# A four-stage transformer kernel: moving sums, centring, decay and gates of its linear attention between engines

## What is computed

```python
xx = xprev - x                                  # x is the layernormed input
mix_in = tanh((x + xx * time_maa_x) @ time_maa_w1)
mrg, mwa, mk_, mv_ = einsum('btfd,fdc->fbtc', mix_in..., time_maa_w2)
xrg = x + xx * (time_maa_rg + mrg)              # and xwa, xk, xv in the same way
r, k, v = xrg @ Wr.T, xk @ Wk.T, xv @ Wv.T
w = -softplus(-(time_decay + tanh(xwa @ decay_w1) @ decay_w2)) - 0.5
g = tanh(xrg @ gate_w1) @ gate_w2
kk = normalise per head (k + tanh(xk @ kkk_w1) @ kkk_w2)
a   = sigmoid(time_aaaaa + xwa @ aaa_w1 @ aaa_w2)
ma  = sigmoid(time_misc_a + xwa @ ma_w1 @ ma_w2)
mk2 = sigmoid(time_misc_k + xk @ mk_w1 @ mk_w2)
k = (k * ma + k * a * (1 - ma)) * exp(min(w * mk2, 0))
S_t = S_{t-1} * diag(exp(w_t)) + (S_{t-1} a_t) b_t^T + v_t k_t^T ;  y_t = S_t r_t
y = groupnorm(y) * ln_w + ln_b + (sum(r * k * faaaa)) * v
out = (y * g) @ Wo.T
```

## Time and profile before

| | us |
|---|---|
| median of 3 runs | 3406.15 |
| lowest, highest | 3391.64, 3433.51 |
| profiled execution, device time | 3376.8 |
| its span, first to last instruction | 3375.1 |

### The profile page before, as it was taken

One profiled execution on the slowest core, in us unless ns is written; L12 is line 12 of the kernel. 1 busy time (PEld: TensorE's weight loads), 2 busy tenths in 40 slices (PEclk: granted clock), 3 DMA queues, 4 the chain that ended last, 5 costly groups with the idle time before them and its releaser, 6 DMA issues.

```text
span 3375.1 us, 99419 instructions
## 1 busy us (share of the span) xinstructions
PE 2913.8 (86%) x42634; PEld 1914.3 (57%) x42634; DVE 2560.1 (76%) x5230; ACT 1876.2 (56%) x3255; POOL 1104.7 (33%) x1294
## 2 busy tenths in 40 slices
PE   6999999998468988988569999999999998599994
PEld 4555555664245555555326565666556566388873
DVE  4677777675748888888657999899999896477774
ACT  3444444444357888888345666656656554166651
POOL 1333333221711222221232443343443332255552
PEclk7999999999789999999778999999999998599996
DMA  7476879100154333342200000000000000156666
GB/s 284 185 281 233 308 289 190 47 2 2 45 179 134 128 126 126 129 135 65 75 1 3 9 11 10 11 13 10 11 10 10 11 13 12 71 211 219 225 221 172
DMA packets 161608, 355.76 MB, mean 105 GB/s; under 512 B 13821, under 2 KB 98559, under 8 KB 154896
## 3 DMA queue, kind: packets, MB, share of 16 engines
q1 hardware_dynamic: 147088, 323.95, 28.2%
q0 software_dynamic: 14080, 25.45, 2.3%
HBM read 136.33 MB, written 216.67 MB: 105 GB/s over the span
## 4 chain that ended last, share of the span: by engine, by line
PE 51%; DVE 25%; ACT 14%; issue 5%; DMA 2%; SPq 1%; POOL 1%; DVEq 0%; POOLq 0%; ACTq 0%
PE ps L1558 6%; PE ps L135 5%; PE ps L137 4%; PE ps L136 4%; PE ps L905 2%; PE ps L346 2%; DVE t L494 2%; ACT t L1044 2%; ACT t L1042 2%; PE ps L912 2%; PE ps L350 2%; PE ps L301 2%; PE ps L307 2%; PE ps L331 2%; DVE t L531 2%
## 5 line engine op out<-in xcount | busy, mean ns | idle before, releaser
L1558 PE MATMUL ps<-t 128*128 128x512 f32 x608 | 325.9, 652 | 56.9 <-DVE t L2072 25.8
L245 POOL TENSOR_SCALAR_AFFINE_SELECT t<-t 128x512 f32<-128x512 f32 x256 | 169.4, 662 | 568.8 <-ACT t L434 568.8
L434 ACT ACTIVATE t<-ps 128x768 f32<-128x768 f32 x256 | 207.1, 809 | 219.4 <-PE ps L333 219.4
L135 PE MATMUL ps<-t 128*128 128x512 f32 (+1 forms) x660 | 276.5, 419 | 36.9 <-DVE t L476 15.1
L494 DVE TENSOR_REDUCE t<-ps 128x2 f32<-128x512 f32 (+1 forms) x512 | 260.4, 550 | 56.6 <-PE ps L307 56.4
L1370 POOL DMA_INDIRECT deltas<-t x92 | 94.4, 1026 | 508.4 <-DVE t L1316 486.3
L137 PE MATMUL ps<-t 128*128 128x512 f32 (+1 forms) x660 | 255.7, 387 | 0.0
L136 PE MATMUL ps<-t 128*128 128x512 f32 (+1 forms) x660 | 255.0, 386 | 0.0
L2825 POOL DMA_INDIRECT answers<-t x156 | 154.1, 988 | 160.0 <-DVE t L2796 122.1
L482 DVE SCALAR_TENSOR_TENSOR t<-t,ps 128x512 fp32r<-128x512 f32 x128 | 95.5, 746 | 129.1 <-ACT t L412 67.6
L1558 PEld LDWEIGHTS ps<-t 128*128 128x128 f32 x608 | 105.0, 197 | 143.0 <-issue 54.5
(11 more groups left out here) (443 smaller groups left out, 8313.1 us busy)
## 6 DMA issues: line engine op xcount, KB each, us to landing
paired<-t SPq DMA_DIRECT2D x14, 8384.0 KB, 38.4
t<-experts SPq DMA_DIRECT2D x39, 1536.0 KB, 6.9
sorted<-t SPq DMA_DIRECT2D x22, 1950.0 KB, 8.9
t<-in_wP SPq DMA_DIRECT2D x92, 320.5 KB, 3.5
experts<-t SPq DMA_DIRECT2D x8, 1536.0 KB, 5.5
t<-sorted SPq DMA_DIRECT2D x39, 260.0 KB, 5.9
t<-answers SPq DMA_DIRECT2D x16, 512.0 KB, 6.9
t<-in_wE SPq DMA_DIRECT2D x8, 768.0 KB, 38.2
```

What stands on the lines that cost most here:

```text
L135: pe.e.matmul(out, a[0], b[0], start=start, stop=False, skip_group_check=True)
L245: pool.e.affine_select(own, own, [[0, 2], [0, 2], [1, 128]], ALU.is_ge, 0.0, base=0, channel_multiplier=-1).then_inc(*kept(b, j))
L434: act.e.activation(pt[:, p, :, :], ps[:, k:k + 2, 0:384], ACT.Exp, scale=float(8 ** -0.5)).then_inc(*prob(b, j))
L1558: pe.e.matmul(ps[out, k, :], lhs, rhs, start=True, stop=True).then_inc(*e_pe(u, name))
```

## The change

- The sum of each mix moves from GpSimd to VectorE. The product with `w` moves there too, joined with a maximum; GpSimd has no E step left.
- Centring (two layernorms, one group norm) becomes part of the product: the weights are identity minus mean. ScalarE copies the centred result out of PSUM and squares it; three 128x512 subtractions of VectorE go.
- The decay of the state becomes a product: ScalarE makes six diagonal matrices a unit, two batches each (12 activations of 128x64, step S0), and TensorE adds `diag S` onto `B S`. VectorE's part of a state step is one sum.
- The seven outputs y are issued together at S7, into one bank, with one sum on VectorE. All seven states are kept.
- The sigmoids' `0.5 t + 0.5` moves from VectorE to ScalarE (3 activations behind the 3 tanh of E13). Smaller joins: softplus' `-0.5` goes into the scale and bias of Ln, the group norm's weight and bias into two three-operand instructions.
- `kk`, `s0`, `s1`, `s2` take 32 rows each, on four different row groups, in place of 128 rows.

`AT`, `HOLD` and the order are unchanged. The core of the diff:

```diff
+                one(u, "kk", w["kw2"][0:32, 0:128], P[9][0:32, :])
+                one(u, "s0", w["waw2"][64:96, 128:256], P[8][64:96, :])
+                one(u, "s1", w["waw2"][96:128, 256:384], P[8][96:128, :])
+                one(u, "s2", w["kw2"][32:64, 128:256], P[9][32:64, :])
 def state(u, s):                                   # PE
+            if 0 <= s <= 5:
                 pe.wait_ge(s_dve, u, "S", s)
+                pe.wait_ge(i_act, 4 * u + 3, "bd")
+                pe.wait_ge(s_act, u, "DG")
                 ... 4 matmuls BN x Sx, then 4 matmuls DG[hr, s, b, :] x Sx[hr, s, b, :]
+            elif s == 6:
+                for ck in range(1, 8):  ... y of chunk ck; one then_inc
 # ACT, E0
+                act.e.activation(xc, ps[:, bank(u, "mean"), :], ACT.Copy)
+                act.e.activation(sq, ps[:, bank(u, "mean"), :], ACT.Square).then_inc(*e_act(u, "sq"))
 # ACT, E13, behind the three tanh
+                for i in range(3):
+                    act.wait_ge(e_act, u, "tanh", i)
+                    act.e.activation(P[5 + i], P[5 + i], ACT.Identity, scale=0.5,
+                                     bias=w["half"]).then_inc(*e_act(u, "sig", i))
 # ACT, S0
+            if s < 0:
+                act.wait_ge(e_dve, u, "G")
+                if u:
+                    act.wait_ge(s_pe, u - 1, "y")
+                gv = G[:, u % 3, :].rearrange("p (b c) -> p b c", b=2)
+                for ck in range(1, 7):
+                    for b in range(2):
+                        m = act.e.activation(DG[:, ck - 1, b, :], w["eye2"], ACT.Copy, scale=gv[:, b, ck:ck + 1])
+                m.then_inc(*s_act(u, "DG"))
 # DVE
+                dve.e.tensor_tensor(P[4 + f], P[4 + f], P[0], ALU.add).then_inc(*e_dve(u, "mix", f))
-                    dve.e.tensor_scalar(P[5 + i], P[5 + i], 0.5, 0.5, ALU.mult, ALU.add)
-                    dve.e.tensor_tensor(nxt, cur, gv[:, :, ck:ck + 1].broadcast_to([128, 2, 64]), ALU.mult)
-                    dve.e.tensor_tensor(nxt, nxt, BN[:, z, ck, :, 0:64], ALU.add)
-                    dve.e.tensor_tensor(nxt, nxt, by(ps[:, k, 0:128], 64), ALU.add)
+                dve.e.tensor_tensor(Sx[:, ck, :, :], BN[:, z, ck, :, 0:64], by(ps[:, k, 0:128], 64), ALU.add)
-                    dve.e.tensor_tensor(yv, yv, by(ps[rows, k, 0:64], 32), ALU.add)       # 14 a unit
+                dve.e.tensor_tensor(yv, yv, by(ps[:, k, :], 256)[:, :, 32:256], ALU.add)  # 1 a unit
 # POOL
-                pool.e.tensor_tensor(P[4 + f], P[4 + f], P[0], ALU.add)
-                pool.e.tensor_tensor(P[7], P[7], P[0], ALU.mult)
```

More of the change, by code:

```diff
@@ L2 @@
 from itertools import islice
+import math
 import numpy as np
@@ new lines, in state @@
+                k = misc.take("s", u, ck)
+                pe.wait_ge(*misc.free("s", u, ck))
+                hold(k, HOLD["s"][s])
+                pe.wait_ge(s_dve, u, "S", s)
+                pe.wait_ge(i_act, 4 * u + 3, "bd")
+                pe.wait_ge(s_act, u, "DG")
+                for b in range(2):
+                    for hr in heads:
+                        pe.e.matmul(ps[hr, k, b * 64:b * 64 + 64], BN[hr, z, ck, b, 64:128], Sx[hr, s, b, :],
+                                    start=(b == 0), stop=False, skip_group_check=True)
@@ new lines, in state @@
+                for b in range(2):
+                    for hr in heads:
+                        m = pe.e.matmul(ps[hr, k, b * 64:b * 64 + 64], DG[hr, s, b, :], Sx[hr, s, b, :],
+                                        start=False, stop=True, skip_group_check=True)
+                m.then_inc(*s_pe(u, "s", ck))
+            elif s == 6:
+                k = misc.take("y", u)
+                pe.wait_ge(s_dve, u, "S", 6)
+                pe.wait_ge(i_act, 4 * u + 3, "q")
+                pe.wait_ge(*misc.free("y", u))
+                for ck in range(1, 8):
+                    for b in range(2):
+                        at = b * 256 + ck * 32
+                        for rows in heads:
+                            m = pe.e.matmul(ps[rows, k, at:at + 32], Sx[rows, ck - 1, b, :], Q[rows, z, at:at + 32],
+                                            start=(ck == 1 and b == 0), stop=True, skip_group_check=True)
+                m.then_inc(*s_pe(u, "y"))
@@ L2077, in feat @@
                 dve.e.scalar_tensor_tensor(out=P[4 + f], in0=bank(f"m{f}"), scalar=w["maa"][:, f + 1:f + 2], in1=P[1],
[L2078 to L2079 removed]
+                                           op0=ALU.add, op1=ALU.mult).then_inc(*e_dve(u, "part", f))
+                misc.give(("e", u, f"m{f}"), e_dve, u, "part", f)
+                dve.wait_ge(e_dve, u, "part", f)
+                dve.e.tensor_tensor(P[4 + f], P[4 + f], P[0], ALU.add).then_inc(*e_dve(u, "mix", f))
             elif s == 10:
@@ L2088, in feat @@
                 misc.give(("e", u, "kk"), e_dve, u, "kk")
-                for i in range(3):
-                    dve.wait_ge(e_act, u, "sig", i)
-                    dve.e.tensor_scalar(P[5 + i], P[5 + i], 0.5, 0.5, ALU.mult, ALU.add).then_inc(*e_dve(u, "sig", i))
             elif s == 14:
                 dve.wait_ge(e_pe, u, "dw")
-                dve.wait_ge(e_pool, u, "mix", 3)
+                dve.wait_ge(e_dve, u, "mix", 3)
                 dve.e.tensor_scalar(P[0], bank("dw"), w["td"], -0.5, ALU.add, ALU.add)
@@ L2234, in state @@
                 if u:
-                    dve.wait_ge(s_pe, u - 1, "y", 7, 1)
+                    dve.wait_ge(s_pe, u - 1, "y")
                 dve.e.tensor_copy(Sx[:, 0, :, :], BN[:, z, 0, :, 0:64]).then_inc(*s_dve(u, "S", 0))
-            elif s <= 6:
+            elif s <= 5:
                 ck = s + 1
[L2239 to L2261, removed]
-                    misc.give(("y", u, ck, h), s_dve, u, "y", ck, h)
```

159 lines of the change are left out of this document (69 added, 90 removed).

## The result

| | median us | lowest | highest | runs |
|---|---|---|---|---|
| before | 3407.06 | 3391.64 | 3433.51 | 4 |
| changed | 3481.46 | 3452.42 | 3533.59 | 4 |

The ratio is 1.018, interval [1.012, 1.024]: the change makes the kernel 1.8% slower, some 62 us, or 3469 on the median before. That is within the 2% that were given the chance of 0.78. The predicted 3410 is missed by 71 us by the median of the four runs, which lies 1.5 us above the upper end of the range, and by 59 by the ratio, which puts it inside. The forecast was for 4 us of loss; the range holds 62 only because it was drawn on to 3480 for a part of rival A. Rival A, the clock, had given 3487 (its 76.7 a unit, added up as the forecast is, with the 4 us of the two ends, makes 3479).

What follows compares the result with a forecast made beforehand. TensorE was taken as the nearly full engine, 65.9 busy of 71.58 us a unit. Forecast 64.2 + 3.9 + 2.4 + 1.0 + 0.5 = 72.0, +6 over 15 periods, -4 at the ends: 3410 us, range 3350 to 3480.

Steps and rivals of the forecast that it cites:

- rival A: TensorE's clock stays low around both waits in each unit: +5 to +6 us a unit, 3487 us; chance 0.15.
- the new wait: TensorE's S1, ahead of the gates, waits for ScalarE's xk evacuation and twelve diagonals: 3.9 us a unit (2.7 to 5.1).
- the price of a diagonal: One 128x64 activation on ScalarE taken at 0.22 us, twelve at 2.6; bounds 1.4 and 3.8.
- The sign it gave for rival A: A granted TensorE clock below 0.95 in mid-stage would show rival A.
- TensorE's work: TensorE's busy time a unit falls from 65.9 to 64.2 us: gates -2.2, outputs -1.2, decay product +1.7.
- The row groups: The four gates on four row groups take 1.3 us in place of 3.5: -2.2 a unit (0 to -2.6).
- ScalarE behind the gates: Three added affine activations before the table load delay L1966; TensorE's next small products wait 2.4 us a unit.
- the clock's term: Two close pauses may lower TensorE's clock for a stretch: 0.5 us a unit added.
- rival B: No pause before the gates: 67.6 us a unit, -4.0, total 3342 us; chance 0.1.
- The scattered ones: TensorE's remaining short pauses, after both VectorE waits go: 1.0 us a unit (0.5 to 1.5).

Runs made afterwards that it cites:

- e2: The changed kernel with the twelve diagonals made earlier, two behind each of steps 1 to 6 of the unit's fourth tile; ratio 0.999 to the kernel before.
- e10: The changed kernel with the twelve diagonals made earlier in the unit, run again on another chip; ratio 0.996 to the kernel before.
- e4: The kernel before with only the twelve diagonal activations added, result unused, and TensorE's S1 waiting for them; ratio 1.029 to the kernel before.
- e6: The changed kernel with the diagonals made early and the sigmoids' half and sum back on VectorE, gates on row groups; ratio 0.988 to the kernel before.
- e3: The changed kernel with four unused products of 512 columns put ahead of TensorE's wait for the diagonals; ratio 1.016 to the kernel before.
- e7: The changed kernel with diagonals early, gates back on 128 rows and the sigmoids' half and sum on VectorE; ratio 0.996 to the kernel before.
- groups 1 and 3: Two of three groups of follow-up runs, each group on one chip beside the kernel before; the changed kernel unaltered measured 1.020 in both.
- e9: The changed kernel unaltered, run again as base on another chip; ratio 1.020 to the kernel before.
- e1: The changed kernel unaltered, as base of the comparisons; ratio 1.020 to the kernel before.

## Why the prediction was right, and where it was wrong

**Right: the new wait decides.** The pause was forecast at 3.9, by S0's place between xk and S1, at 12 x 0.22; measured 4.38, at 2.97 / 12 = 0.25 a diagonal. It stands where it was said, ended by the diagonals. e2, e10 and e4 show from both sides that it costs the change's whole loss or more. The prediction named the price of a diagonal as most likely to be off; it cost only 0.5 us. The sign it gave for rival A, a clock below 0.95 in mid-stage, came too.

**Right: TensorE's work.** 64.2 busy at full clock; 64.3 in e6 at a clock of 0.99. The row groups were taken at 1.3 for the four gates; 1.14 at full clock (e3). The Trainium skill's 3.07 times (TensorE: Matmul & The Clock Gate, "Measured speedup vs the span model") had given 1.14 as well, as an estimate on 3.5; e3 bears it out.

**Half right: ScalarE behind the gates.** Forecast as one wait of 2.4 in each unit. In the unit shown it is 0.76 before `dw` and 1.52 before the small products, 2.3 together; over ten units the second stands in five, and the two come to 1.4 a unit. The first I hadn't seen: `dw` takes the bank of `kk`, four takes back, which VectorE reads. At full clock (e3, e6) VectorE comes to it late, behind ten small instructions and three predicated copies, and the wait is 1.35 to 1.46; in the unit shown it had been idle for 0.7 and waited for `kk` itself. That what row groups give is all given back at ScalarE isn't shown: no pair of runs on one chip compares them with the sigmoids on ScalarE.

**Wrong: the clock's term.** "I add 0.5" was taken from one dip that a unit of before had. In the changed kernel's trace a unit of 77.99 is made of 69.8 busy, 4.4 pause and 3.8 of other waits, against the forecast's 64.7, 3.9 and 3.4. Of the miss of 6.0, 5.1 is busy time, hence clock; 0.5 the pause; 0.4 the rest. Over the whole stage of the same execution the unit is 76.2 and the miss 4.2, of which 3.7 is busy time; the other executions were shorter and have no trace, and 62 us are 4.1 a unit if all of them lie in stage C. Rival A had the mechanism and, with +5 to +6, about the size, and was given 0.15. Its parts differ: up to the gates' end the low clock cost some 1.9 us (2.3 and 2.09 in place of e3's 1.3 and 1.14), not 2.8. The error was to weigh as an accident what a pause of 4 us brings about in every unit. A single dip in a dense stretch prices one dip, not how often it comes nor how much work lies in it. That the total still came inside the range is owed to the range's upper end, not to this term. The Trainium skill's warning of pauses between bursts (the same page, "Why this matters for your kernels") pointed that way, and the trace agrees, 0.50 behind the pause.

**Wrong: rival B's sum.** Without the pause I had 67.6 a unit and 1.9% gain. e2 and e10 are level with the kernel before. Of the 6.3 and 6.5 by which their units stand above the sum, 3.2 and 3.0 are busy time at the low clock, which the kernel before had there too, and 2.7 and 3.0 are pauses without a named cause; the sum had a term for neither. On the one chip that held its clock, e6, which has no wait for ScalarE's sigmoids, still has 68.7 - 64.3 = 4.4 of waits. The scattered ones are the term that was too small: I let them be 1.0. Of the 4.4, 1.3 is the wait before `dw` and some 2.4 are waits under 0.7 for VectorE's mixes and ScalarE's copies; VectorE is busy 55 us of the unit there. So VectorE far from full didn't mean that what TensorE waits for came early.

**Open.** How the clock's price splits into dips by the pause and dips by the thinner work behind it: e3 restored the one and not the total. Why two of the three chips lowered the clock for the variants without a pause (0.93 to 0.94) and the third did not (0.99): they did it for the kernel before too, so the change isn't needed for it; the pauses without a named cause stand in the same two groups, but e4 has next to none of them and the lowest clock, with its own pause. And why stage A, the same code in all, ran at 0.87 in one trace and at 0.97 in another: there is one trace of each run, and the totals shift by up to 64 us with it.

## What to carry to other kernels

When work moves to an idle engine, look where in that engine's queue it lands and who is next in the consumer's queue: twelve small instructions on an engine with 28 us to spare cost 5 us a unit, and made earlier in the unit they stood in no wait of TensorE. Price a new pause of TensorE twice, as time and as the lower clock of the work behind it, and count it in every repetition. A saving on TensorE right before an evacuation on another engine can be worth less than it is long: 2.6 us of busy time shortened the unit by 1.1 (e7 to e6). And before a total is put down to the stage that was changed, look at when that stage starts: here up to 64 us lay before it.

## What the runs showed of the hardware

- Twelve activations of 128x64 from SBUF with a factor per partition take 2.97 us back to back; one lasts 0.33 and the next starts about 0.25 later (e4, the line's durations):

```profile
L2009 ACT ACTIVATE t<-t x192: 332/333/348, 1829.6 to 3066.8; 128x64 f32<-128x64 f32 x192
```

- Four row groups of 32 with 512 columns in f32: eight instructions in 1.14 us at full clock (e3), about 3.2 times faster than whole-array ones (3.69).
- In groups 1 and 3 TensorE paused in each unit of every kernel built from the changed one, 2.7 to 3.5 us in all, for nothing that the profile shows ("issue" in the waits, 1900 to 2700 us). The largest entries of e9, and of e4, which is built from the kernel before and ran on the chip of e1 to e3:

```profile
PE ps L1690 <- issue: 25.2, 41, 1.2
PE ps L1560 <- issue: 7.7, 10, 0.8
PE ps L1632 <- issue: 0.6, 1, 0.6
```

  The second is not one of them: it is the wait of 0.77 before `dw`, at the place where the first trace names VectorE. The others came where GpSimd issues its indirect DMAs. The first trace of the changed kernel has 0.6 us of them at L1690 in ten units, and the ratio to before was the same there (1.018 against 1.020). So they go with the kernel and with the chip or the execution; their cause stays open.
- An execution can have TensorE's products at their lower-level lengths in stages B and C (1166 ns for 592, 5308 us in all) while the recorded clock says 1.00; durations of known products tell it.
